# Scaled input loaded channels first: transposes of the normalised input replaced by a second load and a GpSimd multiply

## The reference, cut to what matters

```python
x = x + xattn(layernorm(x), ctx, ctx, Wq, bq, Wk, bk, Wv, bv, Wo, bo)
x = x + ffn(layernorm(x), W1, b1, W2, b2, expert_W, expert_b)
# xattn: q = queries @ Wq + bq; k, v likewise from ctx; qp = elu(q) + 1, kp = elu(k) + 1
#        out_t = sum over s <= t of (qp_t . kp_s) v_s, per head; divided by cumsum(qp); @ Wo + bo
# ffn:   the expert with the largest logit of a small two-layer net; x @ expert_W[e] + expert_b[e]
```

## Time and profile before

| quantity | value |
|---|---|
| median of 3 runs | 1118.31 us (1118.07 to 1119.86) |
| the profiled execution: its own time | 1114.8 us |
| the profiled execution: span of its instructions | 1113.1 us |
| PE busy | 1033.8 us, 93% of the span |
| DVE busy | 875.7 us, 79% |
| POOL busy | 596.5 us, 54% |
| ACT busy | 458.6 us, 41% |
| mean granted TensorE clock | 0.983 of full speed |

### The profile page before, as it was taken

How to read it: one execution, slowest core, us unless ns; L and a number is a source line. 1 busy time by engine, 2 the same in 40 slices (tenths; PEclk the granted TensorE clock), 3 DMA queues, 4 the chain that set the end, 5 groups by cost and what they waited for, 6 DMA issues and landing times. The chain is left out here.

```text
span 1113.1 us, 38244 instructions
## 1 busy us (share of the span) xinstructions
PE 1033.8 (93%) x15980; PEld 748.6 (67%) x15980; DVE 875.7 (79%) x1908; ACT 458.6 (41%) x741; POOL 596.5 (54%) x546
## 2 busy tenths in 40 slices
PE   3899999999999999999999999999999999988584
PEld 1566666667777677777777677767667777766463
DVE  2588888887878888898888888887888889695442
ACT  1644444444444444444444444444444444421220
POOL 4143445455556655565556646545665455465755
PEclk9999999999999999999999999999999999998888
DMA  3732333342334444433334444323444433241541
GB/s 109 217 112 78 97 97 97 97 116 62 109 120 135 135 125 126 131 93 99 112 126 135 135 116 135 112 74 111 129 135 120 130 105 97 83 147 35 183 142 58
DMA packets 89387, 127.31 MB, mean 114 GB/s; under 512 B 13694, under 2 KB 68609, under 8 KB 89089
## 3 DMA queue, kind: packets, MB, share of 16 engines
q1 hardware_dynamic: 76544, 91.04, 29.5%
q0 software_dynamic: 12672, 33.84, 8.4%
HBM read 73.03 MB, written 36.06 MB: 98 GB/s over the span
## 5 line engine op out<-in xcount | busy, mean ns | idle before, releaser
L611 DVE TENSOR_TENSOR stage<-b_s,causal 128x1024 f32<-128x1024 f32 x192 | 226.2, 1220 | 35.8 <-PE b_s L920 30.9
L444 POOL DMA_INDIRECT buckets<-row,place x128 | 184.2, 1439 | 34.9 <-issue 34.9
L452 POOL DMA_INDIRECT out<-rows x136 | 136.0, 1000 | 58.8 <-issue 44.8
L461 POOL TENSOR_TENSOR onehots<-onehots,onehot 128x32 bf16<-128x32 bf16 x32 | 7.8, 243 | 246.5 <-DVE place L731 246.5
L893 PE MATMUL b_a<-xnT,wq_sb 128*128 128x512 f32 x256 | 127.6, 623 | 6.6 <-ACT x2T L543 4.3
L474 POOL TENSOR_TENSOR x_res<-x_res,bias_o 128x1024 f32<-128x1024 f32 x32 | 84.0, 2624 | 71.7 <-DMA x_res<-in_x 71.7
L893 PE MATMUL b_a<-ctxT,wk_sb 128*128 128x512 f32 x256 | 118.4, 605 | 1.8 <-ACT pos L507 1.8
L898 PE MATMUL b_b<-wo_sb,attT 128*128 128x256 f32 x512 | 118.4, 384 | 0.8 <-DVE attT L808 0.8
L898 PE MATMUL b_b<-wv_sb,ctxT 128*128 128x256 f32 x512 | 119.0, 385 | 0.0
L983 PE MATMUL b_s<-we_sb,x3T 128*128 x464 | 113.1, 389 | 1.0 <-ACT x3T L516 0.8
L898 PEld LDWEIGHTS b_b<-wv_sb,ctxT 128*128 128x128 f32 x512 | 94.7, 190 | 15.8 <-issue 0.5
(11 more groups left out here) (128 smaller groups left out, 1806.6 us busy)
## 6 DMA issues: line engine op xcount, KB each, us to landing
rows<-buckets SPq DMA_DIRECT2D x136, 130.0 KB, 5.2
x_in<-in_x SPq DMA_DIRECT2D x32, 512.0 KB, 5.2
ctxT<-in_ctx SPq DMA_DIRECT2D x32, 512.0 KB, 5.8
qsel<-qp SPq DMA_DIRECT2D x256, 64.0 KB
x_res<-in_x SPq DMA_DIRECT2D x32, 512.0 KB, 6.9
out<-rows POOLq DMA_INDIRECT x136
we_sb<-in_L_ffn_expert_W SPq DMA_DIRECT2D x8, 256.0 KB, 5.9
buckets<-row,place POOLq DMA_INDIRECT x128
```

Source lines behind the costliest of these rows:

```text
L444: pool.indirect_dma_start(buckets, bass.IndirectOffsetOnAxis(place[:, slot(route), t:t + 1], 0), row[:, slot(route), t, :], None).then_inc ...
L452: pool.indirect_dma_start(out.rearrange("t p n -> (t p) n"), bass.IndirectOffsetOnAxis(rows2[:, r, TOKEN:TOKEN + 1].bitcast(U32), 0), rows ...
L611: dve.tensor_tensor(dst.rearrange("p g h s q -> p g (h s) q"), b_s[:, :, 256 * t:256 * t + 256].rearrange("p g (a q) -> p g a q", q=C), ca ...
```

## The change

The host passes `x` a second time, with channels on the partitions (`xT`, 512 KB for each group), as it already does with `ctx`. SP loads this into `x_T` while the group is in stage `load`, after the query product of the group before has been made (`s_q`). `rstd1` no longer multiplies `x_in` on ACT: ACT writes its 512 values to DRAM (`scales`, 16 bytes from each partition) at the end of the step, and reads them back at the start of the next as a row that goes to all 128 partitions (`scale`, 256 KB). POOL then multiplies `x_T` by `scale`, and PE takes `x_T` where it took `xnT`. The transposes of `xn`, ACT's `xn` and ACT's `xnT` are gone. In POOL's step the four scatters to `out` stand behind the product of `z` and `u` (in steps in which a group attends); the multiply stands where they stood. `x_in` is now loaded with four neighbouring tokens on each partition. The ring `rows2` has 15 places in place of 13.

```diff
-    RING = 13
+    RING = 15
+        scales = nc.dram_tensor("scales", (2, N), F32, kind="Internal").ap()
-        xn = sb("xn", [P, GT, D])
-        xnT = sb("xnT", [P, KC, N])
+        scale = sb("scale", [P, N])
+        x_T = sb("x_T", [P, KC, N])
 # SP
-                        sp.wait_ge(s_xn, n(load, 4, -4))
-                    sp.dma_start(x_in[:, slot(load), :, :], of_x(load)).then_inc(s_x[slot(load)], 16)
+                        sp.wait_ge(s_st1, n(load, 4, -4))
+                    sp.dma_start(x_in[:, slot(load), :, :], of_x_tokens(load)).then_inc(s_x[slot(load)], 16)
...
+                if load:
+                    if group_no(load) >= 1:
+                        sp.wait_ge(s_q, n(load, 2))
+                    sp.dma_start(x_T[:, :, :], of_xT(load)).then_inc(s_xT, 16)
 # POOL
-                for quad in (extra_slots_of(j - 1), slots_of(j - 1)):
-                    scatter(quad)
+                if norm:
+                    pool.wait_ge(s_xT, 16 * n(norm, k=1))
+                    pool.wait_ge(s_scale, 16 * n(norm, k=1))
+                    pool.tensor_tensor(x_T[:, :, :], x_T[:, :, :],
+                                       scale[:, :].rearrange("p (o n) -> p o n", o=1).to_broadcast((P, KC, N)),
+                                       ALU.mult).then_inc(s_xs, 1)
                 if merge and j < STEPS - 2:
                     scale2(merge)
+                if not attend:
+                    for quad in (extra_slots_of(j - 1), slots_of(j - 1)):
+                        scatter(quad)
                 if attend:
                     pool.wait_ge(s_zinv, n(attend, k=1))
                     pool.tensor_tensor(z[:, :], z[:, :], u[:, :], ALU.mult).then_inc(s_zprod, 1)
+                    for quad in (extra_slots_of(j - 1), slots_of(j - 1)):
+                        scatter(quad)
 # ACT
+                if norm:
+                    act.wait_ge(s_scales, 16 * n(norm, k=1))
+                    if group_no(norm) >= 1:
+                        act.wait_ge(s_xs, n(norm))
+                    act.dma_start(scale[:, :], scales[slot(norm):slot(norm) + 1, :].to_broadcast((P, N)))\
+                        .then_inc(s_scale, 16)
...
-                if norm:
-                    act.wait_ge(s_xnTp, n(norm, k=1))
-                    if group_no(norm) >= 1:
-                        act.wait_ge(s_q, n(norm, 2))
-                    act.activation(xnT[:, :, :], b_a[:, :, :], ACT.Copy).then_inc(s_xnT, 1)
...
-                    for t in range(GT):
-                        act.activation(xn[:, t, :], x_in[:, slot(load), t, :], ACT.Identity,
-                                       scale=rstd1[:, t:t + 1]).then_inc(s_xn, 1)
+                    act.dma_start(scales[slot(load), :].rearrange("(p c) -> p c", c=GT), rstd1[:, :])\
+                        .then_inc(s_scales, 16)
 # PE
-                if norm:
-                    pe.wait_ge(s_xn, n(norm, 4, 4))
-                    if project:
-                        pe.wait_ge(s_ke, n(project, 4, 4))
-                    turned(b_a, xn).then_inc(s_xnTp, 1)
...
                 if norm:
-                    pe.wait_ge(s_xnT, n(norm, k=1))
+                    pe.wait_ge(s_xs, n(norm, k=1))
                     if merge:
                         pe.wait_ge(s_x2T, n(merge, k=1))
-                    channels_first(b_a[:, 0, :], wq_sb, xnT, 0).then_inc(s_q, 1)
+                    elif project:
+                        pe.wait_ge(s_ke, n(project, 4, 4))
+                    channels_first(b_a[:, 0, :], wq_sb, x_T, 0).then_inc(s_q, 1)
```

More of the change, by code:

```diff
@@ L13, with build @@
 GT = 4
-def build(nc, x, ctx, wq, bq, wk, bk, wv, bv, wo, bo, w1, b1, w2, b2, we, be, out):
+def build(nc, x, xT, ctx, wq, bq, wk, bk, wv, bv, wo, bo, w1, b1, w2, b2, we, be, out):
     TILES, P, D = x.shape
@@ L1101, in step @@
                         pe.wait_ge(s_hT, n(merge, k=1))
-                    channels_first(b_a[:, 1, :], wq_sb, xnT, 1).then_inc(s_q, 1)
+                    channels_first(b_a[:, 1, :], wq_sb, x_T, 1).then_inc(s_q, 1)
                 multiply(slots_of(j)[0:2])
```

28 lines of the change are left out of this document (19 added, 9 removed).

## The result

| | kernel before | changed kernel |
|---|---|---|
| median of the runs | 1119.09 us (4 runs, 1118.07 to 1123.95) | 1104.29 us (4 runs, 1102.61 to 1105.70) |
| profiled execution, its span | 1114.8, 1113.1 us | 1103.39, 1101.6 us |

The ratio is 0.9859, with a 95% interval of 0.9825 to 0.9892. The change is faster by about 15 us. The forecast was 1090, a gain of 28.5. All that follows on parts and steps is read from one execution of each kernel. On the chip of e13, two executions of each kernel ran in a slower state, and its medians leave them out.

A forecast was written before the change was run, and what follows sets the result against it. PE, busy 93% of the span, was taken as the bound. Loop -28.1, start +2.5, step 33 -1.2, tail -2.7 and 1.0 given back made -28.5: from 1118.31 to 1089.8 us, range 1084 to 1109.

The forecast's parts named there:

- What is removed: Loop: PE loses the eight transposes of `xn`, 0.97 us a step, counted 29 times: 28.1 us.
- What TensorE needs, and when: Loop: `late_sums` need `vsel` at +11.66, ready at +11.53; `kp` takes 1.96 us beside POOL's product; no stall seen.
- T: Start time of POOL's multiply, counted from the start of PE's step: +2.2, bounds +1.2 and +6.2.
- The slack of 0.13 us: Loop: time left between the last `vsel`, +11.53, and PE's new demand for it, +11.66.
- the give-back for late factors: Early steps, with a period of only 28.8 us: 1.0 us of the gain given back where the factors come late.
- This distance stays: Loop: ACT issues the factors' write behind the exponential that ends 2.94 us before PE's step starts; this was to hold.
- w + r: Factors' write to DRAM, taken as 2.0 us, plus the read back, 3.0; above 6.1 the prediction would be wrong.
- The rule for the price: Loop: each us the multiply starts past +3.1 costs PE that us, less the slack of 0.13.
- the rival of factors that come late: Loop: late factors stall PE 0.8 us a step, net gain 0.2 in 29 steps, 1111 us; 16 in 100.
- the start, +2.5: Steps 1 to 3 were to lose 2.5 us in all, bounds 0 and +6.
- again some 2: Step 3: `x_T` queued behind the experts' weights and POOL's product behind the multiply, a loss of some 2 us.
- Step 33 and the tail: Step 33: PE's wait for ACT gone, -1.2 us; tail: two more ring places bring loads earlier, -2.7 us.

The follow-up runs named there:

- e13: e3 with the experts' loads one step later still, in step 4: 1230.4 us against 1208.4 of the kernel before on the same chip, ratio 1.0184.
- e3: Changed kernel with the experts' loads issued a step later and POOL's multiply moved behind the product of z and u: 1090.63 us, ratio 0.9765.
- e6: Changed kernel with the slots' scatters back ahead of the row scaling on GpSimd, behind the multiply: 1174.69 us, ratio 1.0485.
- e12: Changed kernel with GpSimd making the factors ahead of the token rows' scatters, not behind: 1130.12 us, ratio 1.0099.
- e4: Changed kernel without the factors' write, read and multiply, so queries lack the first layer norm's 1/std: 1079.64 us, ratio 0.9655.
- e2: Changed kernel with GpSimd's multiply moved behind the row scaling and the product of z and u: 1096.53 us, ratio 0.9802.
- e9: e7 with the factors' write ahead of ScalarE's logarithm and exponential in steps 5 to 8: 1103.02 us, ratio 0.9852.
- e7: Changed kernel with VectorE's input statistics ahead of the centring of the experts' weights in steps 5 to 8: 1106.02 us, ratio 0.9892.
- e5: Changed kernel with 13 places in the ring, as before, in place of 15: 1108.99 us, ratio 0.9910.

## Why the prediction was right and wrong

**What is removed: right, with a smaller size.** 0.97 us were forecast for each of 29 steps. Step 4 gave 1.0 and the 23 middle steps 20.8 us, 0.90 each, with a typical 0.76 and some of the gaps of before gone. The sum moves by up to 5.6 us between kernels with the same middle steps, so the typical one is the better number. The missing 0.2 us lie in the second half of the early sums: 1.08 us there for 0.86. TensorE's own program is the same in e3, e6 and e12, where the group takes 0.91, 0.86 and 0.86, and e4, without the chain, still has 1.08. What differs is the moment of GpSimd's token scatters: they begin 19.6 us into the step in the changed kernel, 21.4 in e12 and 21.9 in e3. Within the changed kernel it shows too: in 15 of the 23 middle steps the fourth scatter starts 0.48 to 0.68 us behind the group's first matmul, and the group takes 1.02 to 1.10 us; in the other 8 none starts there, and it takes 0.86 to 0.88. That the gap goes with the scatters is shown, what in them causes it is not.

**What TensorE needs, and when: right.** The second half of `kp` takes 1.95 to 2.00 us in all 29 steps, the product stands at +7.30, and with T +1.72 there is no wait at `late_sums`. The slack of 0.13 us was enough.

**T: the two terms off, the sum right in the middle.** The write took 1.40 us where 2.0 was taken (up to 3.15 in other middle steps), the read 3.84 where 3.0 was, and the write went out 1.0 us before the exponential ended (492.36 for 493.36), which the prediction named as possible. That +2.2 came out near +1.72 is partly luck: the errors had different signs.

The Trainium skill (DMA: Bandwidth & Descriptors, Specifications) has transfers in pieces below 512 bytes done as read-modify-write. The write of 16-byte pieces landed in 1.40 us here with a DMA share of 0.05 beside it (492.3 to 493.8 us), so no price of it can be seen.

**The step that failed in the loop was the give-back for late factors, 1.0 us.** It was near 4: 3.8 by e2 and 3.6 by e9. "This distance stays" was wrong for the early steps. ScalarE's logarithm waits for the attention output, and the write was issued at -2.21 there, at -3.67 in the middle. The write took 2.48 us and the read 4.28, beside the eight transfers of `qsel`, for 1.40 and 3.84. The sum w + r is 6.76, over the 6.1 that the prediction set as its own mark. The rule for the price held: T +4.70 is 1.60 past +3.1, less the slack of 0.13 is 1.47 us; the waits add up to 1.38, and the period is 1.35 above e2's 27.81. So the rival of factors that come late was true in steps 5 to 10, in full in three of them, and false in the rest.

**The step that failed most was the start, +2.5.** Its first part held: the first query product came 2.95 us later (27.02 for 24.07) and by the third step's keys 1.8 were left (47.21 for 45.39). Step 3 cost 11.4 more where "again some 2" was taken. Only `x_T` was seen behind the experts' loads. The write and the read queued there too, although ScalarE issues them, and the wait for the write held back ScalarE's key activations. The 11.4 us are 7.1 of waits (8.72 for 1.64), 5.3 of a lower clock (3.56, 1.94 and 6.61 us for 1.98, 1.10 and 3.72), less the 0.97 of the transposes. "ACT's wait for the write costs nothing" was true of the loop and not of this step.

The Trainium skill (DMA: Bandwidth & Descriptors, Issuing engines are not separate DMA queues) says that transfers started by different engines run on the same DMA engines and interleave. The trace agrees: 2 KB took 6.75 us behind 3 MB of another engine's queue, and 1.40 alone.

**Step 33 and the tail.** The wait of 1.20 us in step 33 is gone, but a gap of 1.75 us that no engine ended took its place: 28.5 us for 27.9. This gap is 1.1 in e7 and 2.9 in e9, so its size is luck. The tail gave 3.2 us for 2.7; that the ring did it is not settled (e5).

**Together.** -28.5 was forecast and -11.5 came between the two profiles. Start 10.7 less, steps 5 to 9 3.6, the middle 1.5, step 33 1.8, and the tail 0.5 more: 28.5 - 10.7 - 3.6 - 1.5 - 1.8 + 0.5 = 11.4. The medians gave 3.3 us more than the profiles, by the place of the two profiled executions among the others. With the start and the early steps mended, e3 has a start of +2.8 and a time of 1090.63, what was forecast for the change itself; that the numbers agree to 1 us is partly luck, since its gain on its own chip is 26.3 us and its middle step also lacks the gap in the early sums.

## What to carry to other kernels

A small transfer that an engine waits for is priced by what else is in the DMA engines at that moment, whoever issues it; look for bulk loads near it, at the start above all, and at what stands behind its wait in the queue. When an operation is put first on an engine, ask whether anybody needs it first: here it was wanted 11 us later, and one move behind its neighbours made it indifferent to how late its input came. What holds in the middle of a loop has to be worked out again for the steps in which the period is shorter, since the instruction that issues the transfer has other things ahead of it there.

## What was not expected of the hardware

- A DMA of 2 KB from SBUF to DRAM in 16-byte pieces landed 1.40 us after its issue, in less time than any write shown in the earlier trace rows.
- TensorE has gaps of 0.6 to 3.0 us that the profile puts down to no engine. All 62 of them in 14 traces end 2.2 to 2.8 us after a 16 KB packet of the instruction queue began. At one place in step 3 it was 0.81 us in the kernel before, and 2.30 with 3 MB of loads moved beside it.
- Two waits at the start, of 4.06 and 2.89 us, were followed by matmuls that took 2.4 and 2.9 us more than before, by the clock: the granted clock was 1.00 up to 60 us and 0.60 from 60 to 65, and 0.55 over the output product, where it was at the lower of its two levels (0.50, 1.2 GHz) from 75 to 80 us.
- Where GpSimd's indirect scatters fall moved a TensorE group of 64 matmuls by 0.2 us, though the two share no data at that point. On one chip the group beside them took 3.6 us for 0.90.
